# Recurrence of an attention GRU: one transpose for r's tangent and the arguments of candidate and z, and 1-z on VectorE

## The chip, the cores and the metric

One core of a Trainium2 chip. The metric is the device time of the whole program in microseconds. Five engines work side by side in it, each with its own queue of instructions, and they hand over to one another by semaphores: TensorE (PE, and PEld for its weight loads), VectorE (DVE), ScalarE (ACT), GpSimd (POOL) and SyncE (SP), whose queue issues the DMAs.

## What is computed

The program is a residual stack of four layers over x (4 batches x 512 tokens x 128): two kinds of transformer layer, an attention GRU, and a layer of experts that choose their tokens. The change lies in the GRU, which runs 512 steps for 4 batches, each step needing the state of the step before:

```python
def step(h, x_t):
    score = jnp.einsum('bsh,bh->bs', enc_hiddens, h @ W)
    attn = jax.nn.softmax(score, axis=-1)
    context = jnp.einsum('bs,bsh->bh', attn, enc_hiddens)
    gx = jnp.concatenate([x_t, context], axis=-1) @ kernel + bias
    gh = h @ recurrent_kernel
    z = jax.nn.sigmoid(xz + hz)      # xz, xr, xh and hz, hr, hh: the thirds of gx and gh
    r = jax.nn.sigmoid(xr + hr)
    cand = jnp.tanh(xh + r * hh)
    h_new = z * h + (1.0 - z) * cand
    return (h_new, h_new)
```

The sigmoids are written as tangents of half the argument, so 1-z is 0.5 - 0.5 tanh(./2).

## The kernel before, in words

`recurrence` (line 1477) writes one block in which each engine runs a Python-unrolled loop `for t in range(S)` over the 512 steps. The order of the instructions on each engine is the order in which they are written; nothing is planned by a tool. A step is a chain across engines:

- TensorE takes the state (a column per batch) to the scores (L2008), the same scores turned (L2014) and the state's own terms for all gates (L2020). VectorE takes the maximum (L2521) and adds the own terms and the token's terms into `own` (L2527, or L2529 where the token's terms are already in). ScalarE takes the exponential (L2187), TensorE the products with the context tables for r, then for candidate and z (L1758). Here the rows hold four chunks of 32 hidden units times 4 batches, so partition 32 c + b holds chunk c of batch b.
- The tail of the step: VectorE takes a reciprocal (L2531), r's argument `pre_r` (L2534) and the arguments of candidate and z `c_and_z` (L2537). ScalarE takes r's tangent `th_r` (L2190) and z's tangent `th_z` (L2192), both of 32 columns. VectorE makes the candidate's arguments `c_in` by a scan over 64 columns, in which the odd factors are r's tangent and the even ones zero (L2541). ScalarE takes the candidate's tangent `cand` (L2194). VectorE turns z's tangent (L2546) and the candidate (L2548) in blocks of 32 x 32, so that they become columns; ScalarE makes 1-z from the turned tangent (L2196); and a scan over 12 columns, three for each batch, gives the next state (L2552).
- GpSimd writes the old state's terms (L2267) and copies the state to the history (L2271) once the state is there.

Under this chain runs background work of the layers around it, called from each engine's loop at fixed places: of one attention layer (three groups of 128 tokens, 64 units of head pair and batch each; a unit's two heads are scaled one after the other, so 64 scalings of the probabilities on POOL in each group, L2243, over 256, 384 and 512 columns), of the experts behind each group, and in the end the choice of tokens. The stages overlap little: first attention from 1001 to 1235 us, experts to 1393, second attention to 1645, experts to 1802, third attention to 2143, and then experts, choice and bare steps to 2793. POOL's scaling waits, among other things, for the candidate's arguments of the same step (`s_cin`). TensorE's background products stand between the gate products of one step and the scores of the next (`after_gates`), or ahead of the gate products (`ahead_of_gates`).

Ahead of an instruction stand one or more `wait_ge` lines. Three places before the change have two or three: `s_thr, s_precz` ahead of the candidate's scan, `s_thz, s_olds, s_hist` ahead of z's turn, and `s_tc, s_onez` ahead of the state's scan.

Of the kernel before, what the change touches and what calls it, by code (L numbers as in the profile page):

```python
# [16 lines left out]
P = 128  # L17
# [1459 lines left out]
def recurrence(nc, x_t, score_w, gate_w, h_w, x_w, h0_t, spare, x_products, later):  # L1477
# [14 lines left out]
    with ExitStack() as ctx:  # L1492
# [12 lines left out]
        def late_sem(n):  # L1505
# [5 lines left out]
        own = sb("own", 5 * 64)  # L1511
        pre_r, th_r, c_in = sb("pre_r", 32), sb("th_r", 64), sb("c_in", 64)
        c_and_z, pre_z = own[:, 193:320:2], own[:, 257:320:2]
        x_in = spare[:, 0:2 * CHUNK * P].rearrange("p (k t g) -> p k t g", k=2, t=CHUNK)
        x_rows = spare[:, 2 * CHUNK * P:2 * CHUNK * P + 4 * P].rearrange("p (c g) -> p c g", c=4)
        th_z, th_z_t, cand, factors, terms = sb("th_z", 32), sb("th_z_t", 32), sb("cand", 32), sb("factors", 3 * B), sb("terms", 96)
# [8 lines left out]
         s_thz, s_cin, s_cand, s_tz, s_onez, s_tc, s_h, s_olds, s_hist, s_xmm, s_xrow, s_xout) = (  # L1525
            sem(n) for n in ("init", "load", "table", "score", "turnedmm", "ownmm", "rmm", "czmm", "max", "exp", "rt", "own",
                             "prer", "thr", "precz", "thz", "cin", "cand", "tz", "onez", "tc", "h", "olds", "hist", "xmm", "xrow", "xout"))
# [501 lines left out]
        def _(act):  # L2029
# [152 lines left out]
            act.activation(cand[:], th_r[:, 0:32], ACT.Exp).then_inc(s_table, 1)  # L2182
            act.wait_ge(s_table, 1)
            for t in range(S):
# [5 lines left out]
                act.activation(th_r[:, 1:64:2], pre_r[:], ACT.Tanh, scale=0.5).then_inc(s_thr, 1)  # L2190
                act.wait_ge(s_precz, t + 1)
                act.activation(th_z[:], pre_z, ACT.Tanh, scale=0.5).then_inc(s_thz, 1)  # L2192
                act.wait_ge(s_cin, t + 1)
                act.activation(cand[:], c_in[:, 1:64:2], ACT.Tanh).then_inc(s_cand, 1)  # L2194
                act.wait_ge(s_tz, t + 1)
                act.activation(factors[:, 2:3 * B:3], th_z_t[:, 0:B], ACT.Copy, bias=0.5, scale=-0.5).then_inc(s_onez, 1)  # L2196
# [80 lines left out]
        def _(dve):  # L2277
# [220 lines left out]
            dve.memset(th_r[:], 0.0).then_inc(s_init, 1)  # L2498
# [19 lines left out]
            for t in range(S):  # L2518
# [5 lines left out]
                if from_rows(t):  # L2524
                    k = t // CHUNK
                    dve.wait_ge(s_xin[k % 2], 16 * B * sum(from_rows(i * CHUNK) for i in range(k % 2, k + 1, 2)))
                    dve.tensor_tensor(own[:, 0:256:2], ps_own, x_in[:, k % 2, t % CHUNK, :], ALU.add).then_inc(s_own, 1)  # L2527
                else:
                    dve.tensor_copy(own[:, 0:256:2], ps_own).then_inc(s_own, 1)  # L2529
# [4 lines left out]
                dve.scalar_tensor_tensor(out=pre_r[:], in0=ps_r[:, 0:32], scalar=rtotal[:, 0:1], in1=own[:, 0:64:2],  # L2534
                                         op0=ALU.mult, op1=ALU.add).then_inc(s_prer, 1)
                dve.wait_ge(s_czmm, t + 1)
                dve.scalar_tensor_tensor(out=c_and_z, in0=ps_cz, scalar=rtotal[:, 0:1], in1=own[:, 64:192:2],  # L2537
# [497 lines left out]
```

## Time and profile before

| what | us |
|---|---|
| median of 3 runs (lowest, highest) | 2907.86 (2904.52, 2917.85) |
| span of the profiled execution, first to last instruction | 2915.3 |
| PE busy; PEld busy | 2481.6 (85%); 1686.9 (58%) |
| DVE, ACT, POOL busy | 1903.1 (65%), 1576.6 (54%), 991.5 (34%) |
| the recurrence's stretch in it | about 1000 to 2793 |
| mean granted TensorE clock | 0.976 of full speed |

The profiled execution shows nothing around its span but the span itself; it lies 7.4 us above the median of the runs. In a timeline a line is the start, the duration, the engine, the source line, the operation, what it writes and reads, its shape, a count, and in brackets the idle time of the engine before it and what ended it. Idle time "<-issue" is one that the profile shows no release for.

### The profile page before, as it was taken

What the parts mean: (1) busy time and instruction counts of PE and PEld (TensorE: products, weight loads), DVE (VectorE), ACT (ScalarE), POOL (GpSimd) and SP (SyncE); (2) the same over time, 40 slices, a digit from 0 to 9 for tenths busy, and PEclk for the clock granted to TensorE, in tenths of its full rate; (3) what the DMA queues carried; (4) which work ended last, traced back from release to release, by engine and by line L of the source; (5) the groups of instructions that cost most, each with busy time, mean ns of one, the idle gap of its engine ahead of it and who ended that gap; (6) DMA issues with size and microseconds to landing.
All of it is one profiled execution on the core that took longest, in us unless ns stands there. A gap on an engine that the chain in (4) does not pass through costs nothing. (4 is left out here: it accounts for less than half of the span.)

```text
span 2915.3 us, 137471 instructions
## 1 busy us (share of the span) xinstructions
PE 2481.6 (85%) x57411; PEld 1686.9 (58%) x57412; DVE 1903.1 (65%) x7219; ACT 1576.6 (54%) x5266; POOL 991.5 (34%) x1992
## 2 busy tenths in 40 slices
PE   7999999987897799889899898898879877666669
PEld 4666666666455455556565565666656545444448
DVE  4666666775442477767777677777767766776553
ACT  4666666633353366666666576666657543333322
POOL 2000000043010167645677465566636411001125
PEclk9999999999898899999999999999999999999989
DMA  4000000000001200001100011000001000000013
GB/s 150 5 5 5 5 5 8 2 12 1 9 19 46 60 17 18 14 21 42 28 18 17 11 36 35 26 13 14 7 7 35 13 20 7 6 7 7 6 48 85
DMA packets 51896, 64.76 MB, mean 22 GB/s; under 512 B 7432, under 2 KB 36560, under 8 KB 51152
## 3 DMA queue, kind: packets, MB, share of 16 engines
q1 hardware_dynamic: 47184, 50.32, 5.8%
q8 instruction: 454, 7.44, 1.1%
q0 software_dynamic: 4096, 5.67, 1.0%
q14 instruction: 162, 1.33, 0.2%
HBM read 46.38 MB, written 9.60 MB: 19 GB/s over the span
## 5 line engine op out<-in xcount | busy, mean ns | idle before, releaser
L2267 POOL TENSOR_TENSOR gru_terms<-gru_states,gru_signs 128x8 f32<-128x8 f32 x512 | 103.3, 202 | 796.5 <-DVE gru_states L2552 690.2
L2008 PE MATMUL gru_ps_sr<-score_w,gru_states 128*32 128x78 f32 x4096 | 175.4, 243 | 184.0 <-DVE gru_states L2552 174.1
L2187 ACT ACTIVATE gru_p_t<-gru_ps_tc,gru_negmax 128x12 f32<-128x12 f32 x512 | 138.4, 270 | 338.4 <-DVE gru_negmax L2521 319.5
L2190 ACT ACTIVATE gru_th_r<-gru_pre_r 128x32 f32<-128x32 f32 x512 | 119.2, 233 | 303.8 <-DVE gru_pre_r L2534 303.6
L2243 POOL TENSOR_SCALAR bg_probs<-bg_probs,bg_arsum 128x256 f32<-128x256 f32 (+2 forms) x192 | 240.5, 1253 | 84.8 <-DVE gru_c_in L2541 78.7
L1758 PE MATMUL gru_ps_tc<-ctx_gate_w,gru_p_t 128*4 128x64 f32 x12288 | 267.6, 219 | 1.2 <-issue 1.2
L371 ACT ACTIVATE self_probs<-self_sc,self_negmax 128x512 f32<-128x512 f32 x256 | 174.2, 684 | 166.2 <-DVE self_negmax L428 166.2
L1758 PE MATMUL gru_ps_sr<-ctx_gate_w,gru_p_t 128*4 128x34 f32 x12288 | 189.5, 194 | 76.9 <-ACT gru_p_t L2187 74.2
L2008 PEld LDWEIGHTS gru_ps_sr<-score_w,gru_states 128*32 128x32 f32 x4096 | 81.1, 107 | 293.5 <-DVE gru_states L2552 275.6
L1758 PEld LDWEIGHTS gru_ps_sr<-ctx_gate_w,gru_p_t 128*4 128x4 f32 x12288 | 120.2, 86 | 195.4 <-ACT gru_p_t L2187 179.4
L2020 PE MATMUL gru_ps_ox<-late,gru_states 128*4 128x128 f32 x4096 | 225.5, 272 | 0.0
L2521 DVE TENSOR_REDUCE gru_negmax<-gru_ps_sr 128x1 f32<-128x77 f32 x512 | 120.3, 235 | 125.0 <-PE gru_ps_sr L2008 117.4
L2531 DVE RECIPROCAL gru_rtotal<-gru_ps_sr 128x1 f32<-128x1 f32 x512 | 86.1, 168 | 161.4 <-PE gru_ps_sr L1758 157.9
L2541 DVE TENSOR_TENSOR_SCAN gru_c_in<-gru_th_r,gru_own 128x64 f32<-128x64 f32 x512 | 149.4, 292 | 61.9 <-ACT gru_th_r L2190 8.4
L1758 PEld LDWEIGHTS gru_ps_tc<-ctx_gate_w,gru_p_t 128*4 128x4 f32 x12288 | 185.5, 86 | 2.2 <-issue 1.8
L428 DVE TENSOR_REDUCE self_negmax<-self_sc 128x1 f32<-128x512 f32 x256 | 167.3, 685 | 27.4 <-PE self_sc L264 27.4
L211 POOL TENSOR_SCALAR self_n_var<-self_n_mv 128x4 f32<-128x4 f32 x4 | 1.8, 438 | 524.8 <-DVE self_n_mv L457 524.8
L2548 DVE STREAM_TRANSPOSE gru_terms<-gru_cand 128x32 f32<-128x32 f32 x512 | 113.7, 222 | 93.6 <-ACT gru_cand L2194 93.6
L2014 PE MATMUL gru_ps_tc<-gru_states,score_w 128*32 128x1 f32 (+1 forms) x12288 | 170.5, 167 | 0.2 <-issue 0.2
L2194 ACT ACTIVATE gru_cand<-gru_c_in 128x32 f32<-128x32 f32 x512 | 118.3, 231 | 87.4 <-DVE gru_c_in L2541 87.4
L2014 PEld LDWEIGHTS gru_ps_tc<-gru_states,score_w 128*32 128x32 f32 (+1 forms) x12288 | 155.6, 106 | 0.3 <-issue 0.3
L289 PEld LDWEIGHTS self_ot<-self_probs_t,self_v_sb 128*64 128x64 f32 x2048 | 109.6, 136 | 77.7 <-ACT self_probs_t L376 72.1
(417 smaller groups left out, 6599.9 us busy)
## 6 DMA issues: line engine op xcount, KB each, us to landing
bg_w<-in_moe_w SPq DMA_DIRECT2D x48, 256.0 KB, 3.1
bg_wa<-in_wqkv SPq DMA_DIRECT2D x24, 192.0 KB, 2.4
moe_w<-in_moe_w SPq DMA_DIRECT2D x16, 256.0 KB, 3.7
best_w_sb<-in_ec_w SPq DMA_DIRECT2D x16, 256.0 KB
x_products<-late SPq DMA_DIRECT2D x16, 240.0 KB, 2.4
late<-x_products SPq DMA_DIRECT2D x240, 16.0 KB
cross_scratch<-ctab_raw SPq DMA_DIRECT2D x16, 154.0 KB
cross_outs<-cross_scratch POOLq DMA_DIRECT2D x4, 576.0 KB, 5.9
```

Of the source, the lines that this page charges most:

```text
L371: act.activation(probs[:, u % 4, 0:keys(u // 2)], sc[u % 4][:, 0:keys(u // 2)], ACT.Exp, bias=negmax[:, u:u + 1], accum_out=total[:, u:u + ...
L428: dve.tensor_reduce(negmax[:, u:u + 1], sc[u % 4][:, 0:keys(u // 2)], axis=AX.X, op=ALU.max, negate=True).then_inc(s_max, 1)
L1758: last = pe.matmul(bank[32 * c:32 * c + B, 0:hi - lo], p_t[:, B * k:B * k + B], gate_w[:, k, GATE_ALL * c + lo:GATE_ALL * c + hi], start=k ...
L2008: last = pe.matmul(ps_s[32 * b:32 * b + 32, :], state(t)[:, b:b + 1].broadcast_to([P, 32]), score_w[:, b, 0:CTX + 1], start=True, stop=Tru ...
L2014: last = pe.matmul(ps_t[32 * b:32 * b + keys, B * k + b:B * k + b + 1], score_w[:, b, 32 * k:32 * k + keys], state(t)[:, b:b + 1], start=T ...
L2020: last = pe.matmul(ps_own[32 * c:32 * c + B, :], state(t), h_w[:, c, :], start=from_rows(t), stop=True, tile_position=(0, 32 * c), skip_gr ...
L2187: act.activation(p_t[:], ps_t, ACT.Exp, bias=negmax[:, 0:1]).then_inc(s_exp, 1)
L2190: act.activation(th_r[:, 1:64:2], pre_r[:], ACT.Tanh, scale=0.5).then_inc(s_thr, 1)
L2194: act.activation(cand[:], c_in[:, 1:64:2], ACT.Tanh).then_inc(s_cand, 1)
L2243: pool.tensor_scalar(row, row, arsum[:, j:j + 1], None, ALU.mult).then_inc(s_apn, 1)
L2521: dve.tensor_reduce(negmax[:], ps_s[:, 0:CTX], axis=AX.X, op=ALU.max, negate=True).then_inc(s_max, 1)
L2541: dve.tensor_tensor_scan(c_in[:], th_r[:], own[:, 192:256], 0.0, ALU.mult, ALU.add).then_inc(s_cin, 1)
```

## The change

The tangent of r goes into columns 0 to 31 of a tile `gate_rows` of 96 columns, and the arguments of candidate and z into its columns 32 to 95. One transpose turns the 96 columns in blocks of 32 x 32, into every other column of `gate_cols`, ahead of the candidate. The state's own term of the candidate (`own[:, 96:P]`, no longer spaced by two) has a turn of its own into the even columns. The candidate's scan is then over 2 x 4 columns, its tangent over 4 columns straight into `terms`, and z's tangent over 4 columns straight from the turned argument. 1-z is a VectorE instruction and no longer one of ScalarE. The waits for POOL's old terms and history move from the turn of z's tangent to the turn of the own term.

```diff
--- before.py
+++ after.py
@@ -1508,12 +1508,14 @@
         h0, states = sb("h0", B), sb("states", 2 * 3 * B)
         p_t = sb("p_t", 3 * B)
         negmax, rtotal = sb("negmax", 1), sb("rtotal", 1)
-        own = sb("own", 5 * 64)
-        pre_r, th_r, c_in = sb("pre_r", 32), sb("th_r", 64), sb("c_in", 64)
-        c_and_z, pre_z = own[:, 193:320:2], own[:, 257:320:2]
+        own = sb("own", P)
+        pre_r, gate_rows, gate_cols, c_in = sb("pre_r", 32), sb("gate_rows", 96), sb("gate_cols", 192), sb("c_in", 2 * B)
+        th_r, c_and_z = gate_rows[:, 0:32], gate_rows[:, 32:96]
+        gates_turned, own_turned = gate_cols[:, 1:192:2], gate_cols[:, 64:128:2]
+        r_cols, c_cols, z_cols = gate_cols[:, 0:2 * B], gate_cols[:, 64:64 + 2 * B], gate_cols[:, 129:129 + 2 * B:2]
         x_in = spare[:, 0:2 * CHUNK * P].rearrange("p (k t g) -> p k t g", k=2, t=CHUNK)
         x_rows = spare[:, 2 * CHUNK * P:2 * CHUNK * P + 4 * P].rearrange("p (c g) -> p c g", c=4)
-        th_z, th_z_t, cand, factors, terms = sb("th_z", 32), sb("th_z_t", 32), sb("cand", 32), sb("factors", 3 * B), sb("terms", 96)
+        th_z, factors, terms = sb("th_z", B), sb("factors", 3 * B), sb("terms", 3 * B)
         signs = sb("signs", 2 * B)
         fill = sb("fill", 2 * P, BF16)
 
@@ -1522,9 +1524,9 @@
         ps_t, ps_cz = ps_tc[:, 0:3 * B], ps_tc[:, P:P + 64]
         ps_own, ps_x = ps_ox[:, 0:P], ps_ox[:, P:4 * P]
         (s_init, s_load, s_table, s_score, s_turnedmm, s_ownmm, s_rmm, s_czmm, s_max, s_exp, s_rt, s_own, s_prer, s_thr, s_precz,
-         s_thz, s_cin, s_cand, s_tz, s_onez, s_tc, s_h, s_olds, s_hist, s_xmm, s_xrow, s_xout) = (
+         s_thz, s_cin, s_cand, s_hcols, s_gcols, s_onez, s_h, s_olds, s_hist, s_xmm, s_xrow, s_xout) = (
             sem(n) for n in ("init", "load", "table", "score", "turnedmm", "ownmm", "rmm", "czmm", "max", "exp", "rt", "own",
-                             "prer", "thr", "precz", "thz", "cin", "cand", "tz", "onez", "tc", "h", "olds", "hist", "xmm", "xrow", "xout"))
+                             "prer", "thr", "precz", "thz", "cin", "cand", "hcols", "gcols", "onez", "h", "olds", "hist", "xmm", "xrow", "xout"))
         s_xin = [sem(f"xin{i}") for i in range(2)]
 
         h_cols, x, y, g_rows, b_rows, gain, bias, ident = (later[n] for n in (
@@ -2179,7 +2181,7 @@
 
             act.wait_ge(s_init, n_init)
             act.wait_ge(s_b1, 16)
-            act.activation(cand[:], th_r[:, 0:32], ACT.Exp).then_inc(s_table, 1)
+            act.activation(th_z[:], signs[:, 0:B], ACT.Exp).then_inc(s_table, 1)
             act.wait_ge(s_table, 1)
             for t in range(S):
                 act.wait_ge(s_max, t + 1)
@@ -2187,13 +2189,11 @@
                 act.activation(p_t[:], ps_t, ACT.Exp, bias=negmax[:, 0:1]).then_inc(s_exp, 1)
                 after_exp(t)
                 act.wait_ge(s_prer, t + 1)
-                act.activation(th_r[:, 1:64:2], pre_r[:], ACT.Tanh, scale=0.5).then_inc(s_thr, 1)
-                act.wait_ge(s_precz, t + 1)
-                act.activation(th_z[:], pre_z, ACT.Tanh, scale=0.5).then_inc(s_thz, 1)
+                act.activation(th_r, pre_r[:], ACT.Tanh, scale=0.5).then_inc(s_thr, 1)
+                act.wait_ge(s_gcols, t + 1)
+                act.activation(th_z[:], z_cols, ACT.Tanh, scale=0.5).then_inc(s_thz, 1)
                 act.wait_ge(s_cin, t + 1)
-                act.activation(cand[:], c_in[:, 1:64:2], ACT.Tanh).then_inc(s_cand, 1)
-                act.wait_ge(s_tz, t + 1)
-                act.activation(factors[:, 2:3 * B:3], th_z_t[:, 0:B], ACT.Copy, bias=0.5, scale=-0.5).then_inc(s_onez, 1)
+                act.activation(terms[:, 0:3 * B:3], c_in[:, 1:2 * B:2], ACT.Tanh).then_inc(s_cand, 1)
                 after_candidate(t)
 
         @block.gpsimd
@@ -2495,7 +2495,7 @@
             dve.memset(power[:], -0.5).then_inc(s_init, 1)
             dve.memset(inverse[:], -1.0).then_inc(s_init, 1)
             dve.tensor_scalar(q_gain10[:], qk_gain[:, 0:NP], QK_SCALE, None, ALU.mult).then_inc(s_init, 1)
-            dve.memset(th_r[:], 0.0).then_inc(s_init, 1)
+            dve.memset(gate_cols[:], 0.0).then_inc(s_init, 1)
             dve.memset(terms[:], 0.0).then_inc(s_init, 1)
             dve.memset(factors[:, 0:3 * B:3], 0.0)
             dve.memset(factors[:, 1:3 * B:3], 1.0).then_inc(s_init, 1)
@@ -2524,30 +2524,32 @@
                 if from_rows(t):
                     k = t // CHUNK
                     dve.wait_ge(s_xin[k % 2], 16 * B * sum(from_rows(i * CHUNK) for i in range(k % 2, k + 1, 2)))
-                    dve.tensor_tensor(own[:, 0:256:2], ps_own, x_in[:, k % 2, t % CHUNK, :], ALU.add).then_inc(s_own, 1)
+                    dve.tensor_tensor(own[:], ps_own, x_in[:, k % 2, t % CHUNK, :], ALU.add).then_inc(s_own, 1)
                 else:
-                    dve.tensor_copy(own[:, 0:256:2], ps_own).then_inc(s_own, 1)
+                    dve.tensor_copy(own[:], ps_own).then_inc(s_own, 1)
                 dve.wait_ge(s_rmm, t + 1)
                 dve.reciprocal(rtotal[:], ps_total).then_inc(s_rt, 1)
                 dve.wait_ge(s_rt, t + 1)
                 dve.wait_ge(s_own, t + 1)
-                dve.scalar_tensor_tensor(out=pre_r[:], in0=ps_r[:, 0:32], scalar=rtotal[:, 0:1], in1=own[:, 0:64:2],
+                dve.scalar_tensor_tensor(out=pre_r[:], in0=ps_r[:, 0:32], scalar=rtotal[:, 0:1], in1=own[:, 0:32],
                                          op0=ALU.mult, op1=ALU.add).then_inc(s_prer, 1)
                 dve.wait_ge(s_czmm, t + 1)
-                dve.scalar_tensor_tensor(out=c_and_z, in0=ps_cz, scalar=rtotal[:, 0:1], in1=own[:, 64:192:2],
+                dve.scalar_tensor_tensor(out=c_and_z, in0=ps_cz, scalar=rtotal[:, 0:1], in1=own[:, 32:96],
                                          op0=ALU.mult, op1=ALU.add).then_inc(s_precz, 1)
-                dve.wait_ge(s_thr, t + 1)
-                dve.wait_ge(s_precz, t + 1)
-                dve.tensor_tensor_scan(c_in[:], th_r[:], own[:, 192:256], 0.0, ALU.mult, ALU.add).then_inc(s_cin, 1)
-                dve.wait_ge(s_thz, t + 1)
                 dve.wait_ge(s_olds, t + 1)
                 if t:
                     dve.wait_ge(s_hist, t)
-                dve.transpose(th_z_t[:], th_z[:]).then_inc(s_tz, 1)
+                dve.transpose(own_turned, own[:, 96:P]).then_inc(s_hcols, 1)
+                dve.wait_ge(s_precz, t + 1)
+                dve.wait_ge(s_thr, t + 1)
+                dve.transpose(gates_turned, gate_rows[:]).then_inc(s_gcols, 1)
+                dve.wait_ge(s_hcols, t + 1)
+                dve.wait_ge(s_gcols, t + 1)
+                dve.tensor_tensor_scan(c_in[:], r_cols, c_cols, 0.0, ALU.mult, ALU.add).then_inc(s_cin, 1)
+                dve.wait_ge(s_thz, t + 1)
+                dve.tensor_scalar(factors[:, 2:3 * B:3], th_z[:], -0.5, 0.5, ALU.mult, ALU.add).then_inc(s_onez, 1)
+                dve.wait_ge(s_onez, t + 1)
                 dve.wait_ge(s_cand, t + 1)
-                dve.transpose(terms[:, 0:96:3], cand[:]).then_inc(s_tc, 1)
-                dve.wait_ge(s_tc, t + 1)
-                dve.wait_ge(s_onez, t + 1)
                 at = (t + 1) % 2 * 3 * B
                 dve.tensor_tensor_scan(states[:, at:at + 3 * B], factors[:], terms[:, 0:3 * B], 0.0, ALU.mult, ALU.add)\
                    .then_inc(s_h, 1)
```

## Rows read from the trace of the kernel before

**Rows 1.** Timeline, a quiet step; columns: start us, duration us, engine, line, work, idle
```profile
2602.45 0.25 DVE L2534 SCALAR_TENSOR_TENSOR gru_pre_r<-gru_ps_sr,gru_rtotal,gru_own 128x32 f32<-128x32 f32 x1
...
2602.74 0.23 ACT L2190 ACTIVATE gru_th_r<-gru_pre_r 128x32 f32<-128x32 f32 x1 [0.99 <-DVE gru_pre_r L2534]
...
2603.00 0.29 DVE L2541 TENSOR_TENSOR_SCAN gru_c_in<-gru_th_r,gru_own 128x64 f32<-128x64 f32 x1
...
2603.32 0.23 ACT L2194 ACTIVATE gru_cand<-gru_c_in 128x32 f32<-128x32 f32 x1 [0.16 <-DVE gru_c_in L2541]
...
2603.59 0.22 DVE L2548 STREAM_TRANSPOSE gru_terms<-gru_cand 128x32 f32<-128x32 f32 x1 [0.18 <-ACT gru_cand L2194]
2603.84 0.18 DVE L2552 TENSOR_TENSOR_SCAN gru_states<-gru_factors,gru_terms 128x12 f32<-128x12 f32 x1
2604.08 0.16 PEld L2008 LDWEIGHTS gru_ps_sr<-score_w,gru_states 128*32 128x32 f32 x8 [1.09 <-DVE gru_states L2552]
```

**Rows 2.** Waits, last stage (2143 to 2793 us): total us, times, longest us
```profile
PEld gru_ps_sr L2008 <- DVE gru_states L2552: 169.3, 164, 1.8
```

**Rows 3.** Waits, first expert stage (1235 to 1393 us)
```profile
PEld gru_ps_sr L2008 <- DVE gru_states L2552: 15.0, 15, 1.8
```

**Rows 4.** Timeline, a step of the first expert stage
```profile
1319.16 0.18 DVE L2552 TENSOR_TENSOR_SCAN gru_states<-gru_factors,gru_terms 128x12 f32<-128x12 f32 x1
...
1319.47 0.16 PEld L2008 LDWEIGHTS gru_ps_sr<-score_w,gru_states 128*32 128x32 f32 x8
```

**Rows 5.** Timeline, a step of the first attention stage
```profile
1070.50 0.23 ACT L2194 ACTIVATE gru_cand<-gru_c_in 128x32 f32<-128x32 f32 x1 [0.17 <-DVE gru_c_in L2541]
...
1070.64 0.93 POOL L2243 TENSOR_SCALAR bg_probs<-bg_probs,bg_arsum 128x256 f32<-128x256 f32 x1 [0.69 <-DVE gru_c_in L2541]
...
1071.03 0.18 DVE L2552 TENSOR_TENSOR_SCAN gru_states<-gru_factors,gru_terms 128x12 f32<-128x12 f32 x1
...
1071.40 0.16 PEld L2008 LDWEIGHTS gru_ps_sr<-score_w,gru_states 128*32 128x32 f32 x8 [0.17 <-DVE gru_states L2552]
```

**Rows 6.** Timeline, a step of the second attention stage
```profile
1529.07 1.26 POOL L2243 TENSOR_SCALAR bg_probs<-bg_probs,bg_arsum 128x384 f32<-128x384 f32 x1
...
1529.10 0.18 DVE L2552 TENSOR_TENSOR_SCAN gru_states<-gru_factors,gru_terms 128x12 f32<-128x12 f32 x1
...
1529.51 0.16 PEld L2008 LDWEIGHTS gru_ps_sr<-score_w,gru_states 128*32 128x32 f32 x8
```

**Rows 7.** Groups by shape, VectorE, 1040 to 2790 us: busy us, mean ns, idle
```profile
L2362 DVE TENSOR_REDUCE bg_amax<-gru_bg_pair 128x1 f32<-128x512 f32 x64 | 43.0, 672 | 1.0 <-PE gru_bg_pair L1825 1.0
...
L2362 DVE TENSOR_REDUCE bg_amax<-gru_bg_pair 128x1 f32<-128x256 f32 x56 | 22.7, 406 | 0.2 <-issue 0.2
```

**Rows 8.** Timeline, the end of a step of the second attention stage
```profile
1401.13 0.21 ACT L2196 ACTIVATE gru_factors<-gru_th_z_t 128x4 f32<-128x4 f32 x1 [0.17 <-DVE gru_th_z_t L2546]
...
1401.22 1.25 POOL L2243 TENSOR_SCALAR bg_probs<-bg_probs,bg_arsum 128x384 f32<-128x384 f32 x1
...
1401.44 0.40 DVE L2552 TENSOR_TENSOR_SCAN gru_states<-gru_factors,gru_terms 128x12 f32<-128x12 f32 x1 [0.23 <-ACT gru_factors L2196]
```

**Rows 9.** Timeline, a step of the first expert stage whose c-and-z arguments came late
```profile
1240.18 0.28 DVE L2537 SCALAR_TENSOR_TENSOR gru_own<-gru_ps_tc,gru_rtotal,gru_own 128x64 f32<-128x64 f32 x1 [0.19 <-PE gru_ps_tc L1758]
...
1240.57 0.29 DVE L2541 TENSOR_TENSOR_SCAN gru_c_in<-gru_th_r,gru_own 128x64 f32<-128x64 f32 x1
```

**Rows 10.** Waits, the whole recurrence (1000 to 2793 us)
```profile
POOL bg_probs L2243 <- DVE gru_c_in L2541: 78.7, 131, 1.3
```

**Rows 11.** Timeline, the end of a step of the third attention stage
```profile
1821.35 1.57 POOL L2243 TENSOR_SCALAR bg_probs<-bg_probs,bg_arsum 128x512 f32<-128x512 f32 x1
...
1821.44 0.63 DVE L2552 TENSOR_TENSOR_SCAN gru_states<-gru_factors,gru_terms 128x12 f32<-128x12 f32 x1
```

**Rows 12.** Waits, third attention stage (1802 to 2143 us)
```profile
POOL bg_probs L2243 <- DVE gru_c_in L2541: 29.7, 63, 1.0
```

**Rows 13.** Groups by line, third attention stage (1802 to 2143 us)
```profile
L2552 DVE TENSOR_TENSOR_SCAN gru_states<-gru_factors,gru_terms 128x12 f32<-128x12 f32 x96 | 27.2, 283 | 4.3 <-ACT gru_factors L2196 0.9 <-DVE gru_terms L2548 0.3
```

## What the change was predicted to do

> **What bounds the kernel now.** I read the page's busy shares first and found no bound in them: every engine rests a good part of the time, because 512 steps of a recurrence, each waiting for the one before, fill the stretch from 1000 to 2793 us. So the step is the unit. In the timeline of a step with nothing heavy beside it [rows 1], one instruction hands to the next across engines: r's argument (2602.45), its tangent on ScalarE, the candidate's scan, the candidate's tangent, the transpose, the state scan (2603.84), and TensorE's score weights at 2604.08. From r's argument to the start of the state scan it is 1.39 us: 0.29 + 0.26 + 0.32 + 0.27 + 0.25. Each link is the duration of one instruction plus a gap of 0.03 to 0.04. This tail is what the change rewrites.
>
> Then I asked in which steps the tail sets the step. TensorE's loads wait for the state in 164 steps of the last stage [rows 2], but in only 15 of the first expert stage [rows 3]; elsewhere TensorE is still at background work. In an expert step the load follows the state's end by 0.13 [rows 4], against 0.06 in rows 1: TensorE is 0.07 behind. In the first attention stage (steps whose POOL scaling waits for the candidate's arguments) it is 0.19 after, so 0.13 to 0.14 behind [rows 5]; in the second, in steps where POOL starts late for another reason, 0.23 after, so 0.17 to 0.18 behind [rows 6]. What the tail loses below that costs nothing there.
>
> **The change, part by part.** Removed from the tail: the transpose of the candidate (0.22 and a gap of 0.03 [rows 1]). Removed elsewhere: the turn of z's tangent and ScalarE's 1-z, both beside other work. Added on VectorE: the turn of the own terms (32 columns, about 0.20), which fits between the c-and-z arguments and the end of r's tangent, since POOL's old terms and history are ready long before; I cost it at nothing, and if POOL were late it would hold r's turn behind it by that lateness. Added on the path: one transpose of 96 columns ahead of the candidate. 1-z becomes a VectorE instruction that starts when z's tangent ends; z's four columns start on ScalarE beside the candidate's scan, so 1-z is done some 0.1 before the candidate's tangent. Nothing.
>
> *The long transpose.* No row has 96 columns. Floor: 0.22, as for 32 [rows 1]. Ceiling: 64 more columns at the scan's rate, (0.29 - 0.18)/52 = 2.1 ns each [rows 1], which gives 0.36. The nearest in kind is a one-input stream of one element per step: the maximum takes 406 ns for 256 and 672 for 512 [rows 7], 1.04 ns each, so 0.22 + 64 x 1.04 ns = 0.29. I take 0.29. (The Trainium skill, VectorE: DVE Perf Modes, section "The three transpose paths", has 311 ns for 128 by 128 in bf16; less 32 columns of a 0.96 GHz clock that is an estimate of 0.28, and the sum would fall by some 5 us.)
>
> *The order of the waits.* The code writes several waits ahead of one instruction, and the trace tells the places apart. Where the late one is written first, the gap is 0.03: r's tangent to the candidate's scan [rows 1], whose waits are "thr, precz". Where the late one is written second, it is 0.10: in one step ScalarE's 1-z was last, ended at 1401.34 and the state scan, whose waits are "tc, onez", began at 1401.44 [rows 8]; in another the c-and-z arguments ended at 1240.46 (1240.18 + 0.28, rounded) and the candidate's scan began at 1240.57 [rows 9], both on VectorE itself. In the changed code the late wait stands second three times on the path: "precz, thr" ahead of the long transpose, "hcols, gcols" ahead of the candidate's scan, "onez, cand" ahead of the state scan. So three links get 0.10 and not 0.03. The bounds are 0.03 and 0.10; I take 0.10, which both rows with the late wait second show.
>
> The Trainium skill speaks differently: VectorE: DVE Perf Modes, section "The DRAIN you can't avoid", has eight copies take the same time with a semaphore after each as with one at the end, so that "the semaphore costs nothing extra here". By that rule the three links would stay at 0.03; it is the first rival below.
>
> *The new tail.* 0.29 (to r's tangent) + 0.23 (tangent) + 0.10 + 0.29 (long transpose) + 0.10 + 0.17 (a scan of 8: 0.18 for 12, less 4 x 2.1 ns) + 0.03 + 0.21 (a tangent of 4 columns, as 1-z when it had to wait [rows 8]) + 0.10 = 1.52, against 1.39. The state scan starts 0.13 later in a plain step.
>
> *POOL's scaling of the probabilities.* POOL starts it on the end of the candidate's scan: cand's tangent at 1070.50 follows that end by 0.03, POOL at 1070.64, so 0.17 after the end [rows 5]; 131 of the 192 scalings wait for it [rows 10]. While POOL reads, the state scan is held: with 512 columns the scan that began 0.09 after POOL ended 0.72 after POOL's start (0.63 long, against 0.18) [rows 11], with 384 columns one that began 0.22 after ended 0.62 after it [rows 8], and one that began 0.03 after POOL was not held [rows 6]. With 256 columns I extrapolate 0.51. So in these steps the state ends a fixed time after POOL's start, hence after the candidate's scan, which moves from 0.84 (0.29 + 0.26 + 0.29) to 0.29 + 0.23 + 0.10 + 0.29 + 0.10 + 0.17 = 1.18: the state is 0.34 later with 384 and 512 columns. With 256 it ends today unheld at 1.39 + 0.18 = 1.57 and then at 1.18 + 0.17 + 0.51 = 1.86: 0.29 later. In the other scaling steps, whose POOL start I leave where it is, the scan falls into the hold anew (start 0.17 after POOL instead of 0.03): 0.29 and 0.39 later.
>
> *The sum.*
> - Last stage: 164 steps x 0.13 = 21.3; 28 more (650 us hold some 192) x (0.13 - 0.07) = 1.7. Together 23.
> - Two expert stages of some 158 us, 44 steps each: 2 x 15 x 0.13 + 2 x 29 x 0.06 = 7.4.
> - Third attention stage: 63 scalings wait for the candidate's scan, and the state scan's mean is 283 ns there over 96 instructions [rows 12, 13]: 63 x 0.34 + 33 x 0.13 = 25.7.
> - First attention stage, 64 scalings, 0.29 later, TensorE 0.14 behind: 64 x 0.15 = 9.6. Second, 64: the 34 or so that wait 0.34, the 30 others 0.39, TensorE 0.18 behind: 34 x 0.16 + 30 x 0.21 = 11.7. (131 - 63 = 68 waiting ones, taken as halves.)
>
> That is 77 us. The profiled execution spans 2915.3 us, 7.4 above the median of the runs and inside their spread, so the difference is put on the median: 2907.86 + 77 = 2985.
>
> **The rivals.**
> 1. *The order of the waits is free* (0.03 each). Speaks for it: the gap of 0.03 is the rule in rows 1. Against it: rows 8 and 9. The tail is 1.32, 0.07 shorter; (164 + 30 + 33) x 0.07 = 16 is gained, but the 63 held steps lose 0.21, as the candidate's scan still ends 0.21 later (1.05 against 0.84): 13. Result -3: 2905.
> 2. *The other side: the scan slips ahead of POOL's hold.* It decides at a start between 0.03 (not held [rows 6]) and 0.09 (held [rows 11]) after POOL's. With free waits the scan starts 0.03 + 0.21 + 0.03 - 0.17 = 0.10 after POOL, so it needs some 0.05 more, for instance from a tangent of four columns shorter than 0.21. Then the 63 steps, which today end at 0.84 + 0.17 + 0.72 = 1.73, end at 1.32 + 0.18 = 1.50: 63 x 0.23 = 14, with the 16 a gain of 30: 2878.
> 3. *The long transpose streams at the scan's rate*, 0.36: 0.07 more in all steps but those that TensorE covers, some 420: 29 more, 3014. Speaks for it: a transpose must take in before it gives out. Against it: the 32-column one takes 0.20 to 0.22, hardly more than a scan of 12.
> 4. *The hold doesn't grow*, because POOL reads at other times than I read out of four rows: all steps lose 0.13 alone, the 63 nothing (1.52 + 0.18 = 1.70 against 1.73): 77 less 63 x 0.34 less 14 of the 21 in the first two stages is 42: 2950.
>
> **How the numbers follow.** Forecast 0.71; rival 1 0.06; rival 2 0.04; rival 3 0.11; rival 4 0.08. The range holds the forecast with the transpose's floor (0.07 x 420 = 29 less: 2956) and ceiling, and rivals 3 and 4: 2950 to 3016. Half a per cent, 14.5 us, is about what a measurement of this kernel can tell from no change. Slower: forecast, 3 and 4, 0.90; the same: rival 1, 0.06; faster: rival 2, 0.04.
>
> **What would show it.** In the changed trace, in a quiet step: the gap from r's tangent to the long transpose, from that to the candidate's scan and from the candidate's tangent to the state scan 0.10 each (0.03: rival 1); the transpose 0.29 (0.36: rival 3); steps of 3.43 instead of 3.30. In the third attention stage the state scan's mean well above 283 ns and most held scans ending 0.72 after POOL's start; a mean near 183 is rival 2 or 4. I am wrong altogether if the late wait, though written second, is answered in 0.03, or if TensorE's background work turns out to cover the tail in the last stage too.

## The result

The changed kernel takes 2985.39 us (median; 2985.07 to 2986.0), the kernel before 2909.43 (2904.52 to 2917.85, one run more than the forecast had). The ratio is 1.0247, with a 95% interval of 1.0233 to 1.0261: slower by 2.5%. The forecast was 2985, in a range of 2950 to 3016.

| | before | after |
|---|---|---|
| span of the profiled execution, us | 2915.3 | 2983.3 |
| first state scan of the recurrence starts, us | 1001.4 | 1001.5 |
| last state scan starts, us | 2792.8 | 2868.2 |

The recurrence has become 75.3 us longer, and the medians stand 76.0 apart. The spans differ by less, 68.0, because what follows the recurrence took 7.4 longer in the profiled execution of before (122.5 us; 114 to 115 in all the other traces here); the change doesn't touch that.

The timeline of a quiet step of after, last stage, answers to [rows 1] (start us, duration us, engine, line, work, idle before and its releaser):

```profile
2671.21 0.25 DVE L2534 SCALAR_TENSOR_TENSOR gru_pre_r<-gru_ps_sr,gru_rtotal,gru_own 128x32 f32<-128x32 f32 x1
...
2671.49 0.23 ACT L2192 ACTIVATE gru_gate_rows<-gru_pre_r 128x32 f32<-128x32 f32 x1 [0.99 <-DVE gru_pre_r L2534]
...
2671.83 0.28 DVE L2545 STREAM_TRANSPOSE gru_gate_cols<-gru_gate_rows 128x96 f32<-128x96 f32 x1
2672.14 0.20 ACT L2194 ACTIVATE gru_th_z<-gru_gate_cols 128x4 f32<-128x4 f32 x1 [0.42 <-DVE gru_gate_cols L2545]
2672.21 0.17 DVE L2548 TENSOR_TENSOR_SCAN gru_c_in<-gru_gate_cols 128x8 f32<-128x8 f32 x1
2672.38 0.17 DVE L2550 TENSOR_SCALAR gru_factors<-gru_th_z 128x4 f32<-128x4 f32 x1
2672.41 0.21 ACT L2196 ACTIVATE gru_terms<-gru_c_in 128x4 f32<-128x4 f32 x1
2672.72 0.18 DVE L2554 TENSOR_TENSOR_SCAN gru_states<-gru_factors,gru_terms 128x12 f32<-128x12 f32 x1 [0.18 <-ACT gru_terms L2196]
```

From r's argument (2671.21) to the state scan (2672.72) it is 1.51; before it was 1.39. The long transpose ends at 2672.11. ScalarE, which waits for it alone, starts z's tangent 0.03 later; VectorE, which waits for two things and has the late one written second, starts the candidate's scan 0.10 later, though the transpose was its own. The same 0.10 stands in front of the transpose (the tangent ends at 2671.72) and of the state scan (the candidate ends at 2672.62).

Waits of after (us in total, times, longest), first in the last stage, as [rows 2], then in the third attention stage, as [rows 12]:

```profile
PEld gru_ps_sr L2010 <- DVE gru_states L2554: 194.0, 189, 1.9
...
POOL bg_probs L2243 <- DVE gru_c_in L2548: 51.2, 64, 1.5
```

TensorE waits for the state in 189 of the 192 steps of the last stage, where it was 164, and POOL for the candidate's scan in 64 scalings of the third, where it was 63. Now the steps with a POOL scaling, one of each attention stage, in the timeline:

```profile
1061.26 0.93 POOL L2243 TENSOR_SCALAR bg_probs<-bg_probs,bg_arsum 128x256 f32<-128x256 f32 x1 [1.00 <-DVE gru_c_in L2548]
1061.43 0.34 DVE L2554 TENSOR_TENSOR_SCAN gru_states<-gru_factors,gru_terms 128x12 f32<-128x12 f32 x1 [0.18 <-ACT gru_terms L2196]
...
1503.06 1.25 POOL L2243 TENSOR_SCALAR bg_probs<-bg_probs,bg_arsum 128x384 f32<-128x384 f32 x1 [1.00 <-DVE gru_c_in L2548]
1503.24 0.44 DVE L2554 TENSOR_TENSOR_SCAN gru_states<-gru_factors,gru_terms 128x12 f32<-128x12 f32 x1 [0.18 <-ACT gru_terms L2196]
...
1901.21 1.57 POOL L2243 TENSOR_SCALAR bg_probs<-bg_probs,bg_arsum 128x512 f32<-128x512 f32 x1 [0.84 <-DVE gru_c_in L2548]
1901.38 0.55 DVE L2554 TENSOR_TENSOR_SCAN gru_states<-gru_factors,gru_terms 128x12 f32<-128x12 f32 x1 [0.18 <-ACT gru_terms L2196]
```

The state scan starts 0.17 to 0.18 after POOL in all three and is held: it takes 0.34, 0.44 and 0.55 instead of 0.18, and ends 0.51, 0.62 and 0.72 after POOL's start. Before, no state scan of the first stage was held ([rows 5] is one of its 64 steps with a scaling). Over the third attention stage the group of after answers to [rows 13] (busy us, mean ns, idle before and what ended it):

```profile
L2554 DVE TENSOR_TENSOR_SCAN gru_states<-gru_factors,gru_terms 128x12 f32<-128x12 f32 x96 | 40.6, 423 | 17.3 <-ACT gru_terms L2196 17.3
```

The mean went from 283 to 423 ns. By stage, from one state scan to the next, summed over the steps of each stage (the last four columns: kernels of the experiments against the same trace of before, in short names):

| stage | forecast, us | after | late first | before, late second | joint | joint, POOL later |
|---|---|---|---|---|---|---|
| first attention | +9.6 | +16.6 | +3.2 | +9.1 | +2.0 | +2.8 |
| second attention | +11.7 | +6.5 | +1.5 | +2.4 | +2.2 | +1.1 |
| both expert stages | +7.4 | +6.5 | -0.1 | +5.8 | -1.3 | -2.4 |
| third attention | +25.7 | +24.7 | +10.6 | +10.5 | +10.0 | -9.1 |
| last | +23 | +21.1 | -2.4 | +22.4 | -13.6 | -14.2 |
| sum | +77 | +75.3 | +12.8 | +50.2 | -0.8 | -21.6 |

Executions differ by a few us ahead of and behind the recurrence; that is not in this table, and it is in the ratios.

### The profile page after: what moved, and what is told of

Read it like the earlier page. It is cut to its first block and busy times, and to the rows that moved or that the text cites. A ratio compares the mean times of both kernels' runs of the same rounds, so it can differ in the third digit from the quotient of the medians.

```text
span 2983.3 us, 137982 instructions
## 1 busy us (share of the span) xinstructions
PE 2490.2 (83%) x57411; PEld 1689.1 (57%) x57412; DVE 1995.0 (67%) x7731; ACT 1516.3 (51%) x4754; POOL 990.8 (33%) x1992
## 5 line engine op out<-in xcount | busy, mean ns | idle before, releaser
L2192 ACT ACTIVATE gru_gate_rows<-gru_pre_r 128x32 f32<-128x32 f32 x512 | 117.3, 229 | 297.2 <-DVE gru_pre_r L2534 297.1
L2194 ACT ACTIVATE gru_th_z<-gru_gate_cols 128x4 f32<-128x4 f32 x512 | 105.2, 205 | 215.5 <-DVE gru_gate_cols L2545 215.5
L2554 DVE TENSOR_TENSOR_SCAN gru_states<-gru_factors,gru_terms 128x12 f32<-128x12 f32 x512 | 142.5, 278 | 92.9 <-ACT gru_terms L2196 92.8
L2545 DVE STREAM_TRANSPOSE gru_gate_cols<-gru_gate_rows 128x96 f32<-128x96 f32 x512 | 142.8, 279 | 30.0 <-ACT gru_gate_rows L2192 2.9
```

What stands on the lines that cost most here:

```text
L2192: act.activation(th_r, pre_r[:], ACT.Tanh, scale=0.5).then_inc(s_thr, 1)
L2545: dve.transpose(gates_turned, gate_rows[:]).then_inc(s_gcols, 1)
L2554: dve.tensor_tensor_scan(states[:, at:at + 3 * B], factors[:], terms[:, 0:3 * B], 0.0, ALU.mult, ALU.add)\
```

## The experiments

Two causes were claimed: the place of the late wait, and POOL's hold on the state scan. The first group of four kernels shared a chip on which the kernel before took 2915.0 us, the second group of four one on which it took 2915.04.

**Late wait first.** The changed kernel, with each of the three pairs of waits turned round:

```diff
-                dve.wait_ge(s_precz, t + 1)
                 dve.wait_ge(s_thr, t + 1)
+                dve.wait_ge(s_precz, t + 1)
...
-                dve.wait_ge(s_hcols, t + 1)
                 dve.wait_ge(s_gcols, t + 1)
+                dve.wait_ge(s_hcols, t + 1)
...
-                dve.wait_ge(s_onez, t + 1)
                 dve.wait_ge(s_cand, t + 1)
+                dve.wait_ge(s_onez, t + 1)
```

> The changed kernel with the two waits swapped at three places, so that the late one is written first: thr before precz, gcols before hcols, cand before onez. No operation and no data path differs. Theory (the place of the late wait costs 0.07 us a link): the gaps r's tangent to long transpose, long transpose to candidate's scan, candidate's tangent to state scan fall from 0.10 to 0.03 each, the tail from 1.51 to 1.31 us, a quiet step from 3.42 to 3.22. The steps whose state scan POOL holds lose 0.07 x 2 only, since POOL still starts 0.17 after the candidate's scan. Sum by the steps as before: about 9 below the kernel before, 2900 us (2890 to 2910). If the state scan, now about 0.10 after POOL's start, escapes the hold: 2875. Rival (the loss lies in the operations, the long transpose and the added instructions): no change, 2985, gaps still 0.10.

Measured: 2929.36 us, ratio 1.0051 (1.0033 to 1.0068). Swapping lines gave back 0.0196 of 2915, some 57 of the 72 us that the change costs, but some 24 less than I expected. A quiet step of it in the timeline:

```profile
2615.58 0.23 ACT L2192 ACTIVATE gru_gate_rows<-gru_pre_r 128x32 f32<-128x32 f32 x1 [0.99 <-DVE gru_pre_r L2534]
...
2615.84 0.28 DVE L2545 STREAM_TRANSPOSE gru_gate_cols<-gru_gate_rows 128x96 f32<-128x96 f32 x1
...
2616.15 0.20 ACT L2194 ACTIVATE gru_th_z<-gru_gate_cols 128x4 f32<-128x4 f32 x1 [0.35 <-DVE gru_gate_cols L2545]
2616.15 0.17 DVE L2548 TENSOR_TENSOR_SCAN gru_c_in<-gru_gate_cols 128x8 f32<-128x8 f32 x1
2616.36 0.21 ACT L2196 ACTIVATE gru_terms<-gru_c_in 128x4 f32<-128x4 f32 x1
2616.39 0.17 DVE L2550 TENSOR_SCALAR gru_factors<-gru_th_z 128x4 f32<-128x4 f32 x1
2616.66 0.18 DVE L2554 TENSOR_TENSOR_SCAN gru_states<-gru_factors,gru_terms 128x12 f32<-128x12 f32 x1
```

The gaps ahead of the long transpose and of the candidate's scan fell to 0.03. The third didn't. The candidate's scan came earlier by 0.07 against z's tangent, so 1-z, which waits for both VectorE and z's tangent, no longer ends 0.07 before the candidate (2616.57) but only 0.01 (2616.56). Its wait now stands second, and the state scan starts 0.10 behind it (2616.66). "1-z is done some 0.1 before" holds, roughly, only in the kernel with the late waits, which delay the candidate and not z. The third gap makes some 13.6 of the missing 24 (the sums of this kernel and of the one with joint semaphores in the table, +12.8 and -0.8); the rest is not traced to a step here.

**The kernel before, with its late waits second.** The same price, paid by the old order of work:

```diff
-                dve.wait_ge(s_thr, t + 1)
                 dve.wait_ge(s_precz, t + 1)
+                dve.wait_ge(s_thr, t + 1)
...
-                dve.wait_ge(s_tc, t + 1)
                 dve.wait_ge(s_onez, t + 1)
+                dve.wait_ge(s_tc, t + 1)
```

> The kernel before, with the two waits swapped at two places, so that the late one is written second: precz before thr ahead of the candidate's scan, onez before tc ahead of the state scan. None of the change's operations is in it. Theory: two links of the tail go from 0.03 to 0.10, the tail from 1.39 to 1.53, quiet steps from 3.30 to 3.44, and the steps whose POOL scaling starts late lose more, because their state scan falls into POOL's hold (0.30 to 0.40). Sum over the steps: 62 us more, 2970 (2950 to 2985). Rival (the order of waits is free): 2908.

Measured: 2961.65 us, ratio 1.0153 (1.0136 to 1.017). Two swapped pairs of lines and nothing else cost 1.5%. A quiet step of it:

```profile
2668.35 0.23 ACT L2190 ACTIVATE gru_th_r<-gru_pre_r 128x32 f32<-128x32 f32 x1 [0.99 <-DVE gru_pre_r L2534]
...
2668.68 0.29 DVE L2541 TENSOR_TENSOR_SCAN gru_c_in<-gru_th_r,gru_own 128x64 f32<-128x64 f32 x1 [0.17 <-ACT gru_th_r L2190]
...
2669.27 0.22 DVE L2548 STREAM_TRANSPOSE gru_terms<-gru_cand 128x32 f32<-128x32 f32 x1 [0.19 <-ACT gru_cand L2194]
2669.59 0.18 DVE L2552 TENSOR_TENSOR_SCAN gru_states<-gru_factors,gru_terms 128x12 f32<-128x12 f32 x1
```

Both gaps are 0.10 (2668.58 to 2668.68, 2669.49 to 2669.59) where they were 0.03 [rows 1]. The last stage pays 22.4 us for 192 steps, 0.12 a step. By the ratio the total is some 45 us where 62 were expected. The smallest share is the second attention stage's, +2.4 in 66 steps; the expectation has no sums by stage to set beside the table, so where the rest is missing stays open.

**POOL's scaling later, third stage.** The changed kernel; in the third attention stage POOL starts the scaling when the new state is there, and not on the candidate's scan, so it can't read beside the state scan:

```diff
-                pool.wait_ge(s_cin, t + 1)
+                pool.wait_ge(*((s_h, t + 2) if g == 3 else (s_cin, t + 1)))
```

> The changed kernel, in which POOL's scaling of the probabilities in the third attention group (512 columns) waits for the step's new state instead of the candidate's arguments; the first two groups stay. Theory (POOL's read holds the state scan): in the third stage the state scan takes 0.18 again instead of 0.55 in the 63 steps, its mean there falls from 423 to 183 ns, the state comes 0.37 earlier in them, of which TensorE or the next maximum take little: 22 us less, 2963 (2958 to 2970). Price: the scaling ends about 0.5 later in the step; TensorE turns those probabilities over a step later, so nothing. Rival (the state scan's length has another cause): no change, or slower by the later scaling.

Measured: 2975.39 us, ratio 1.0203 (1.0186 to 1.022), some 13 us under after by the ratios, where 22 were expected. The third stage's sum fell by 17.5, from +24.7 to +7.2, the other stages stayed as in after within 0.5. Its state scan in that stage:

```profile
L2554 DVE TENSOR_TENSOR_SCAN gru_states<-gru_factors,gru_terms 128x12 f32<-128x12 f32 x97 | 17.7, 183 | 17.4 <-ACT gru_terms L2196 17.4
```

No scan is held any more. The scans are 23 us shorter together ((423 - 183) x 96), of which 17.5 came through.

**Both, and POOL later in half of the other scalings.** Late waits first, as above, and the scaling on the new state in the third stage and, elsewhere, for the first of a unit's two heads (a group has 32 units of head pair and batch, not 64, and so 64 scalings):

```diff
-                pool.wait_ge(s_cin, t + 1)
+                pool.wait_ge(*((s_h, t + 2) if g == 3 or j == 0 else (s_cin, t + 1)))
```

> The changed kernel with the late wait first at the three places, and POOL's scaling held for the new state in the third group and for the first head of a unit in the first two groups. Theory: no link of 0.10 is left and no state scan is held; the tail is 1.31 (0.08 under the kernel before), 227 plain steps gain that, 63 steps of the third stage 0.23 to 0.24. Sum over the steps: 36 below the kernel before, 2873 us (2862 to 2885), the lowest of these. If the later scaling delays TensorE in the first two stages, 2880 to 2890. Rival (the tail is not the bound once it is shorter, because background work of ScalarE, which starts later than before, sets the exponential): 2895 to 2908.

Measured: 2917.65 us, ratio 1.0008 (0.9999 to 1.0018): a miss by 45 us. The third stage gained as meant (-6.4 against before), but the second attention stage lost 7.2 and the first 5.3, although only 4 and 3 scans are held there, and the last gained only 1.0: 1-z again ends with the candidate, as in the kernel with the late wait first, and stands second. Waits of TensorE for the scaled probabilities in the second attention stage, this kernel's:

```profile
PEld gru_bg_turn L1836 <- POOL bg_probs L2243: 15.6, 29, 1.6
PE gru_bg_turn L1836 <- POOL bg_probs L2243: 7.4, 23, 1.3
```

and those of before:

```profile
PEld gru_bg_turn L1834 <- POOL bg_probs L2243: 11.8, 30, 1.3
PE gru_bg_turn L1834 <- POOL bg_probs L2243: 1.7, 2, 1.0
```

TensorE's matmuls wait for the scaled probabilities 23 times instead of 2. Against the kernel with the late waits first, the state scans of this stage are 9.3 us shorter together, but from the state's end to TensorE's score weights it is 8.4 longer, and from the exponential to the reciprocal, where TensorE's gate products lie, 5.5. So here the hold is exchanged for lateness of TensorE that costs more; the waits above show a part of it.

**One semaphore for each pair.** The changed kernel, with both producers of a pair counting up one semaphore and VectorE waiting for two counts in one wait. The order of waits is gone as a cause, and which of 1-z and the candidate is late no longer matters (the lines cut out change the other producers to `s_gcols` and `s_cand` in the same way):

```diff
-                act.wait_ge(s_gcols, t + 1)
+                act.wait_ge(s_gcols, 2 * t + 2)
...
-...then_inc(s_precz, 1)
+...then_inc(s_thr, 1)
...
-                dve.wait_ge(s_precz, t + 1)
-                dve.wait_ge(s_thr, t + 1)
+                dve.wait_ge(s_thr, 2 * t + 2)
...
-                dve.wait_ge(s_hcols, t + 1)
-                dve.wait_ge(s_gcols, t + 1)
+                dve.wait_ge(s_gcols, 2 * t + 2)
...
-                dve.wait_ge(s_onez, t + 1)
-                dve.wait_ge(s_cand, t + 1)
+                dve.wait_ge(s_cand, 2 * t + 2)
```

> The changed kernel with one semaphore in the place of two at the three places: the c-and-z arguments and r's tangent raise one, both transposes another, 1-z and the candidate's tangent a third, and each waiting instruction waits for twice the count of steps. So no instruction of the tail waits for two. Theory (each second wait that ends last costs 0.07; in the run with the late wait first, 1-z had become the late one, written second): all three gaps 0.03, the tail 1.31 us where that run has 1.37 and the changed kernel 1.51; a quiet step 3.22. Steps held by POOL gain nothing on that run, some 260 others 0.065: 17 us less within the recurrence, so 4 us under the kernel before, a ratio of 0.9985 (0.995 to 1.002). Rival (the transposes and the tangent bound the tail at 1.37 whatever the waits): a ratio of 1.005 as in that run.

Measured: 2911.36 us, ratio 0.9988 (0.9976 to 1.0). A quiet step, and a step of the third attention stage:

```profile
2640.68 0.25 DVE L2534 SCALAR_TENSOR_TENSOR gru_pre_r<-gru_ps_sr,gru_rtotal,gru_own 128x32 f32<-128x32 f32 x1
...
2640.97 0.23 ACT L2192 ACTIVATE gru_gate_rows<-gru_pre_r 128x32 f32<-128x32 f32 x1 [0.99 <-DVE gru_pre_r L2534]
...
2641.23 0.28 DVE L2544 STREAM_TRANSPOSE gru_gate_cols<-gru_gate_rows 128x96 f32<-128x96 f32 x1
...
2641.54 0.17 DVE L2546 TENSOR_TENSOR_SCAN gru_c_in<-gru_gate_cols 128x8 f32<-128x8 f32 x1
2641.75 0.21 ACT L2196 ACTIVATE gru_terms<-gru_c_in 128x4 f32<-128x4 f32 x1
2641.78 0.17 DVE L2548 TENSOR_SCALAR gru_factors<-gru_th_z 128x4 f32<-128x4 f32 x1
2641.99 0.18 DVE L2551 TENSOR_TENSOR_SCAN gru_states<-gru_factors,gru_terms 128x12 f32<-128x12 f32 x1
...
1902.37 1.57 POOL L2243 TENSOR_SCALAR bg_probs<-bg_probs,bg_arsum 128x512 f32<-128x512 f32 x1 [0.63 <-DVE gru_c_in L2546]
1902.47 0.62 DVE L2551 TENSOR_TENSOR_SCAN gru_states<-gru_factors,gru_terms 128x12 f32<-128x12 f32 x1
```

All three gaps are 0.03, the state scan follows the candidate's end (2641.96) by that, and the tail is 1.31 from r's argument. So the price of the late waits in this change is the whole of its loss: 0.0259 of the time, some 75 us. The interval reaches 1.0: against the kernel before this one is the same. The hold is still there: the scan that starts 0.10 after POOL ends 0.72 after it, and the third stage is still 10 us over before.

**The same, with POOL later in the third stage.** Both edits shown above.

> The same with one semaphore in the place of two, and POOL's scaling in the third attention group (512 columns) waiting for the step's new state. Theory: the state scan's mean in the third stage falls to 183 ns, and that stage from some 10 us above the kernel before to some 10 below it; with the shorter tail in the plain steps the recurrence takes 25 us less than the kernel before: ratio 0.991 (0.988 to 0.995), faster than both kernels. Rival (the later scaling costs TensorE what the hold cost): ratio 0.998.

Measured: 2890.56 us, ratio 0.992 (0.9903 to 0.9938): faster than the kernel before by 0.8%, and the only one here that is clearly faster than both. The third stage went from +10.0 to -9.1. A step of it:

```profile
1900.91 0.18 DVE L2551 TENSOR_TENSOR_SCAN gru_states<-gru_factors,gru_terms 128x12 f32<-128x12 f32 x1
...
1901.27 1.58 POOL L2243 TENSOR_SCALAR bg_probs<-bg_probs,bg_arsum 128x512 f32<-128x512 f32 x1 [1.08 <-DVE gru_states L2551]
```

**The kernel before, with POOL later in the third stage.** The edit of the third experiment on the old order of work.

> The kernel before with that one line alone: POOL's scaling in the third attention group waits for the step's new state. Theory: the state scan's mean in the third stage falls from 283 to 183 ns, 63 steps save 0.15: 10 us less, ratio 0.9966 (0.994 to 0.999). It tells how much of the run with both belongs to the hold and how much to the change itself. Rival: nothing, 1.000.

Measured: 2911.17 us, ratio 0.999 (0.9979 to 1.0002). The mean of the state scan fell from 283 to 183 ns, which is 9.6 us over 96 steps, but the stage gained only 4.5, and the ratio's interval reaches 1.0. The start times show where the other half went: the first 17 steps of the stage became 3.2 us longer, the other 79 gained 7.7. In those first steps the time from the state's end to TensorE's score weights grew by 2.0 together, and in two of them r's argument and the state scan moved apart by 0.9 each, because ScalarE, ahead of r's tangent, waits for a shift that POOL makes right behind the scaling. The waits of the third stage, before and then here:

```profile
ACT bg_xn L2051 <- POOL bg_shift L2216: 2.3, 2, 1.2
...
ACT bg_xn L2051 <- POOL bg_shift L2216: 4.1, 2, 2.1
```

What makes TensorE late in those steps is not shown. Neither edit alone gives what both give: 0.9988 for the joint semaphores, 0.999 for the later scaling, 0.992 together.

**1-z back on ScalarE.** The kernel with joint semaphores, and 1-z again on ScalarE, behind the candidate's tangent:

```diff
                 act.activation(terms[:, 0:3 * B:3], c_in[:, 1:2 * B:2], ACT.Tanh).then_inc(s_cand, 1)
+                act.wait_ge(s_thz, t + 1)
+                act.activation(factors[:, 2:3 * B:3], th_z[:], ACT.Copy, bias=0.5, scale=-0.5).then_inc(s_cand, 1)
...
-                dve.wait_ge(s_thz, t + 1)
-                dve.tensor_scalar(factors[:, 2:3 * B:3], th_z[:], -0.5, 0.5, ALU.mult, ALU.add).then_inc(s_cand, 1)
```

> The run with one semaphore in the place of two, with 1-z back on ScalarE, behind the candidate's tangent, from z's tangent as it stands in columns: one part of the change undone. Theory: ScalarE issues it 0.13 behind the candidate's tangent and takes 0.19 to 0.21, so it ends 0.11 after that tangent and the state scan starts 0.11 later: tail 1.42, quiet steps 3.33, 25 us over that run, ratio 1.007 (1.004 to 1.010). Rival (1-z is hidden on ScalarE as in the kernel before): no difference from that run.

Measured: 2933.92 us, ratio 1.0051 (1.0034 to 1.0067), 0.63% or some 18 us over the kernel with 1-z on VectorE. A quiet step:

```profile
2661.60 0.21 ACT L2196 ACTIVATE gru_terms<-gru_c_in 128x4 f32<-128x4 f32 x1
2661.71 0.19 ACT L2198 ACTIVATE gru_factors<-gru_th_z 128x4 f32<-128x4 f32 x1
2661.94 0.18 DVE L2551 TENSOR_TENSOR_SCAN gru_states<-gru_factors,gru_terms 128x12 f32<-128x12 f32 x1 [0.37 <-ACT gru_factors L2198]
```

1-z ends at 2661.90, 0.09 after the candidate (2661.81), and the state scan waits for it. VectorE's 1-z is a part of the change that earns its place, once the waits are joined.

## Why the prediction was right

*The order of the waits* is the step that decided, and it held in size: three gaps of 0.10, and the tail 1.51 where 1.52 was worked out. That it is the place of the wait, and not the new instructions, is shown from both sides: put first, two of the gaps fell to 0.03 at the same work; put second in the old kernel, two gaps rose to 0.10; joined, all three fell. The rule of the Trainium skill weighed there (VectorE: DVE Perf Modes, "The DRAIN you can't avoid": no extra cost for a semaphore after each of eight copies) doesn't carry over to two waits ahead of one instruction: the traces here have 0.03 behind a single wait, after a VectorE instruction as after another engine's, and 0.10 behind a wait that stands second and ends last.

*Rival 1* named what the change is worth without that price, 2905 or 3 us under before. The kernel with joint semaphores is that case, and came 0.0012, some 3.5 us, under before (interval to 1.0). Its parts were near: +10.0 in the third stage (63 x 0.21 less 33 x 0.07 is 10.9) against a gain of 13.6 in the last (164 x 0.07 is 11.5); the first two attention stages, which it put at nothing, lost 4.2. Rival 2 asked for a state scan that slips ahead of the hold; with cheap waits it starts 0.10 after POOL, as worked out there, and is held.

*The long transpose* took 0.28 (forecast 0.29): rival 3 is out. *1-z* was hidden as the forecast said, but by less than "some 0.1": it ends at 2672.55, 0.07 before the candidate. With cheaper waits the cover is gone, which is a part of the miss in two experiments.

*POOL's hold* ended 0.51, 0.62 and 0.72 after POOL's start, the first of them extrapolated. Rival 4 is out: the third stage has +24.7, where that rival would give 33 x 0.13 = 4.3 and the tail alone in every step 96 x 0.12 = 11.5, and with the scaling moved past the state scan it has +7.2.

*What was mis-sized* is how far behind TensorE is in the first two attention stages, and the two errors, +7.0 and -5.2, nearly cancel: that the sum came out within 2 us is luck to that extent. In the first I put it 0.14 behind in all 64 steps with a scaling, from one step [rows 5]. The rows of before for the next scaling step, and for the step of the second stage ahead of the one in [rows 6]:

```profile
1074.47 0.18 DVE L2552 TENSOR_TENSOR_SCAN gru_states<-gru_factors,gru_terms 128x12 f32<-128x12 f32 x1
1074.70 0.16 PEld L2008 LDWEIGHTS gru_ps_sr<-score_w,gru_states 128*32 128x32 f32 x8 [0.27 <-DVE gru_states L2552]
...
1525.44 0.23 DVE L2552 TENSOR_TENSOR_SCAN gru_states<-gru_factors,gru_terms 128x12 f32<-128x12 f32 x1
...
1526.04 0.16 PEld L2008 LDWEIGHTS gru_ps_sr<-score_w,gru_states 128*32 128x32 f32 x8 [0.17 <-issue]
```

The steps alternate, as a unit of attention work takes two steps there. In the first stage some 35 of the 64 loads follow the state by 0.05, so TensorE waits and the full 0.29 is lost there: 35 x 0.29 + 29 x 0.15 = 14.5, against 16.6 measured for the whole stage. In the second, 28 follow it by 0.37 or more, so TensorE is at least 0.32 behind there. Summed over the steps of a stage (tail: from r's argument to the state's end; cover: what TensorE's lateness takes of that), in us:

| stage | tail later: forecast | measured | cover: forecast | measured |
|---|---|---|---|---|
| first attention | 64 x 0.29 = 18.6 | 19.5 | 64 x 0.14 = 9.0 | 3.2 |
| second attention | 34 x 0.34 + 30 x 0.39 = 23.3 | 21.9 | 64 x 0.18 = 11.5 | 16.0 |

So the hold and the tail were right in both and the cover was wrong in both. The measured cover is the fall of the time from the state's end to TensorE's score weights, 9.4 to 6.2 and 20.8 to 7.7; in the second stage 2.9 more were in TensorE's gate products, from the exponential to the reciprocal (60.7 to 57.8), which [rows 6] couldn't show. One step stood for a pattern of two.

## What to carry to other kernels

Where an instruction on the path waits for two things, write the wait for the one that ends last first, if the other has ended well before (0.01 wasn't enough here, 0.07 was), or let both producers count up one semaphore; a step that chains three such pairs 512 times lost 2.5% to it here, and joining them is the safer cure, since the late one can change. When a chain is rewritten, look at what another engine starts on the moved link: here POOL's scaling hung on the candidate's scan and followed it into the state scan. And read as many neighbouring steps as the pattern has phases before multiplying one by the count.

## What the runs showed of the hardware

A second wait is an instruction of its own. The first line of the page of after, and of the kernel with joint semaphores:

```profile
span 2983.3 us, 137982 instructions
```

```profile
span 2908.6 us, 136446 instructions
```

That is 1536 fewer, three for each of 512 steps, with the same work on every engine (7731 instructions of VectorE in both). That this instruction's own handling makes the 0.07 is argued, not shown.

The wait that stands second needn't end last to cost. In the quiet step of the kernel with the late wait first, 1-z ends 0.01 before the candidate, and the state scan still begins 0.10 behind 1-z. In the step of [rows 1] the c-and-z arguments, which stand second, end at 2602.90, 0.07 before r's tangent, and cost nothing:

```profile
2602.62 0.28 DVE L2537 SCALAR_TENSOR_TENSOR gru_own<-gru_ps_tc,gru_rtotal,gru_own 128x64 f32<-128x64 f32 x1
```

POOL's scaling keeps VectorE's state scan (two inputs in SBUF) waiting until 0.51, 0.62 and 0.72 us after POOL's start for 256, 384 and 512 columns; with 512 the end is the same for a scan that comes 0.10 and one that comes 0.17 after POOL. POOL's own spans are longer: 0.93, 1.25 and 1.57. The candidate's transposes of before, with one input, are not held: 131 of them start within a scaling and take 222 ns on average, as the 381 others do. The Trainium skill (SBUF — State Buffer, "SBUF: two separate sides") has VectorE, with two SBUF inputs, and GpSimd take turns at a shared pair of ports, the loser blocked for the whole instruction; the traces show the turn, but a scan that begins 0.03 after POOL is not held [rows 6], and the hold ends at less than six tenths of POOL's instruction. POOL's spans are rough in this profile, so it stays open which part of its instruction the hold covers.
